# Output projection of a gated delta rule: two heads summed in PSUM, transposes moved from TensorE to a DMA

## The reference, cut to what matters

```python
H, DK, DV = 16, 96, 192
_, o = jax.lax.scan(step, S0, xs)          # o: (B, T, H, DV)
gate = (hidden_states @ Wg).reshape(B, T, H, DV)
var = jnp.mean(o * o, axis=-1, keepdims=True)
o = o * jax.lax.rsqrt(var + EPS) * norm_weight * jax.nn.silu(gate)
return o.reshape(B, T, VAL_DIM) @ Wo       # (B, T, 3072) @ (3072, 512), added to x
```

## Time and profile before

| | busy, us | share of the span |
|---|---|---|
| PE | 2216.2 | 96% |
| PE weight loads | 1536.5 | 66% |
| DVE | 2069.4 | 90% |
| ACT | 1463.5 | 63% |
| POOL | 1061.0 | 46% |
| DMA (share of the 16 engines) | | 20.3% |

### The profile page before, as it was taken

The page is one execution under the profiler, slowest core; times in us unless marked ns, Lnnn a source line. Parts: engine busy times, 40 slices in busy tenths (PEclk is TensorE's granted clock), DMA queues, the critical chain, the costliest instruction groups (busy, mean ns, idle before and its releaser), DMA issues. The chain is left out here.

```text
span 2311.0 us, 60628 instructions
## 1 busy us (share of the span) xinstructions
PE 2216.2 (96%) x22433; PEld 1536.5 (66%) x22456; DVE 2069.4 (90%) x4515; ACT 1463.5 (63%) x4019; POOL 1061.0 (46%) x1542
## 2 busy tenths in 40 slices
PE   5899999999999999999999999999999999888998
PEld 3576767676776767676767676767677676763554
DVE  8899999999999999999999999999999989567886
ACT  4566666666666666767677677766656566424665
POOL 3535445444535454545454544544443545224564
PEclk9999999999999999999999999999999999897999
DMA  5212222222222222222222222221111111021000
GB/s 140 61 39 55 54 58 51 58 55 55 53 53 55 53 50 60 65 66 64 59 60 51 64 61 67 58 66 39 39 36 35 23 34 23 18 87 59 21 24 28
DMA packets 289411, 121.07 MB, mean 52 GB/s; under 512 B 211510, under 2 KB 267094, under 8 KB 288604
## 3 DMA queue, kind: packets, MB, share of 16 engines
q1 hardware_dynamic: 289116, 117.19, 19.7%
HBM read 85.40 MB, written 31.74 MB: 51 GB/s over the span
## 5 line engine op out<-in xcount | busy, mean ns | idle before, releaser
L1445 DVE SCALAR_TENSOR_TENSOR d_y<-bank,d_cw,d_y 128x508 f32<-128x508 f32 (+2 forms) x576 | 421.4, 732 | 6.2 <-ACT d_y L1199 1.3
L791 POOL TENSOR_SCALAR d_ms<-d_sso 128x4 f32<-128x4 f32 x64 | 14.6, 228 | 573.9 <-ACT d_junk L1338 573.9
L740 POOL TENSOR_TENSOR d_Gm<-cst,gh 128x512 f16<-128x512 f32 x128 | 130.6, 1041 | 184.5 <-DVE d_ohl L1614 184.4
L1619 DVE SCALAR_TENSOR_TENSOR x<-bank,x 128x512 f32<-128x512 f32 x256 | 172.1, 677 | 47.3 <-PE bank L1012 47.3
L1199 ACT ACTIVATE d_y<-bank,d_cw 128x512 f32<-128x512 f32 x192 | 131.1, 684 | 77.6 <-PE bank L857 75.3
L1323 ACT ACTIVATE d_thg<-bank 128x384 f32<-128x384 f32 x128 | 62.3, 487 | 178.9 <-PE bank L967 176.6
L821 POOL TENSOR_SCALAR d_K<-d_tok,d_Em 128x96 f32<-128x96 f32 x256 | 156.9, 628 | 0.1
L1206 ACT ACTIVATE d_th<-d_y 128x512 f32<-128x512 f32 x192 | 121.8, 635 | 46.2 <-DVE d_y L1451 35.2
L775 POOL TENSOR_TENSOR d_V<-d_tok,d_kinv 128x640 f32<-128x640 f32 (+1 forms) x128 | 125.8, 1003 | 41.9 <-issue 39.1
L1248 ACT ACTIVATE d_tok<-bank 128x384 f32<-128x384 f32 x256 | 125.7, 491 | 24.3 <-PE bank L873 20.6
L1466 DVE SCALAR_TENSOR_TENSOR d_yv<-d_th,d_y 128x512 f32<-128x512 f32 x128 | 89.0, 696 | 52.7 <-ACT d_th L1206 44.5
(11 more groups left out here) (340 smaller groups left out, 6881.5 us busy)
## 6 DMA issues: line engine op xcount, KB each, us to landing
lt_blocks<-d_LT SPq DMA_DIRECT2D x64, 256.0 KB, 2.5
d_fw<-turned_gate_w SPq DMA_DIRECT2D x32, 256.0 KB, 3.2
d_XT<-x_blocks SPq DMA_DIRECT2D x128, 64.0 KB, 2.4
d_X<-x_blocks SPq DMA_DIRECT2D x128, 64.0 KB, 2.4
d_fw<-turned_val_w SPq DMA_DIRECT2D x32, 256.0 KB, 3.1
d_fw<-turned_out_w SPq DMA_DIRECT2D x32, 256.0 KB, 2.8
d_st<-in_L_attn_Wg_dram SPq DMA_DIRECT2D x16, 384.0 KB, 3.9
ternary<-d_ft SPq DMA_DIRECT2D x48, 128.0 KB, 1.9
```

Of the source, the lines that this page charges most:

```text
L740: nc.gpsimd.tensor_tensor(Gm[:, w, :, :], over(U, 1, B), over(gh[:, w, n, :], 2, P), ALU.mult).then_inc(s["Gm_ready"], 1)
L1445: nc.vector.scalar_tensor_tensor(out=yy[:, :, tap:], in0=pp[:, :, 0:P - tap], scalar=cw[:, ds(st.kp, 1), t, 3 - tap], in1=yy[:, :, tap:], ...
L1619: nc.vector.scalar_tensor_tensor(out=xs, in0=bank[(4, 7, 6, 5)[i]][:, :], scalar=1.0 / (SO * SW), in1=xs, op0=ALU.mult, op1=ALU.add).then_ ...
```

## The change

Steps are paired. Two heads (2j and 2j + 1) share a chunk of output, and their 384 columns are cut in three groups of 128 instead of twice 128 + 64; both heads are summed in PSUM. A unit `u` is a pair of heads, a chunk and two of the four batches: 64 units in all, each 2 batches x 3 groups x 3 products = 18 matmuls and two adds of 128x512. `units(n)` says which are done in step n: none for n < 6, unit n - 6 for n = 6 to 59, two (54 and 55) in step 60, and two in each of the steps 61 to 64. `wo` holds three groups of rows instead of two, and is kept for a pair.

The transposes go by way of DRAM. `low` is one instruction now; SP's `store` writes `ohl` to `normed` after it, and `load` reads a unit back with one transposing DMA of 128 x 1536 f16 into `onT`, which now has two buffers. In steps 5 to 59 it loads the unit of the next step (unit 55 goes out at the start of step 60). From step 61 on, it loads both units of the same step, behind the store of that step. The 12 transposes on PE and the two copies on ACT are gone. To make room, POOL's product `UB` is written into `Em` directly.

```diff
-        "wo": [[sb(f"wo{q}{h}", [P, 2, D], F16) for h in "hl"] for q in range(2)],
-        "nw": sb("nw", [P, 2]),
...
         "img": [nc.dram_tensor(f"x_blocks{q}", (N_BLOCK * I_STRIDE,), F32).ap() for q in range(2)],
...
+def wo_rows(k):
+
+    return (0, P, slice(0, HB)) if k % 2 == 0 else (HB, 0, slice(HB, P))
+
+
+N_PAIR = H // 2
+PER_PAIR = 2 * CH
+LAST = NS - CH + 1
+
+
+def units(n):
+
+    if n < 6 or n > NS:
+        return []
+    if n >= LAST:
+        first = (N_PAIR - 1) * PER_PAIR + 2 * (n - LAST)
+        return [first, first + 1]
+    return [n - 6, n - 5] if n == LAST - 1 else [n - 6]
+
+
+def added(n):
+
+    return max((2 * u + 2 for u in units(n)), default=0)
+
+
+def loads(n):
+
+    if n >= LAST:
+        return units(n)
+    return units(n + 1)[0:1] if n + 1 < LAST else []
+
+
+def stored_at(u):
+
+    return PER_PAIR * (u // PER_PAIR) + CH + 1 + u % PER_PAIR // 2
 
 
...
                         src = src.rearrange("(b x) -> b x", b=B)[:, at:at + HB * HB].rearrange("b (p e) -> p b e", p=HB)
                         sp.dma_start(tile, src).then_inc(s["X_loaded"], 16)
 
+            def store(n):
+
+                k, c = (n - 1) // CH, (n - 1) % CH
+                past(sp, "low_ready", n)
+                for q in range(2):
+                    past(sp, f"onT_in{q}", 16 * CH * (k // 2 - 1))
+                dst = oh[k // 2 % 2][c].rearrange("p (g h v) -> p g h v", h=2, v=DV)[:, :, k % 2, :]
+                sp.dma_start(dst, ohl[:, :, :, :].rearrange("p b l v -> p (b l) v")).then_inc(s["oh_out"], 16)
+
+            def load(u):
+
+                c, half = u % PER_PAIR // 2, u % 2
+                past(sp, "oh_out", 16 * stored_at(u))
+                past(sp, "wo_done", 2 * u - 2)
+                w = 2 * 6 * P
+                sp.dma_start_transpose(onT[u % 2][:, :, :], oh[u // PER_PAIR % 2][c][:, half * w:(half + 1) * w]).then_inc(s[f"onT_in{u % 2}"], 16)
...
                     gather(st)
-                    for place in range(2):
-                        for i in done_jobs(st, place):
-                            next_weights(i + 1)
+                    for i in done_jobs(st, 0):
+                        next_weights(i + 1)
+                if st.output:
+                    store(st.n)
+                    for u in loads(st.n):
+                        load(u)
+                if st.turn:
+                    for i in done_jobs(st, 1):
+                        next_weights(i + 1)
                     scatter(st)
...
-                nc.gpsimd.tensor_tensor(UB[:, :, :], over(cst[:, C_NU:C_NU + P], 1, B), over(Dn[:, :], 2, P), ALU.mult).then_inc(s["kappa_done"], 1)
+                past(pool, "PT_ready", m - 1)
+                nc.gpsimd.tensor_tensor(Em[q][:, :, :], over(cst[:, C_NU:C_NU + P], 1, B), over(Dn[:, :], 2, P), ALU.mult).then_inc(s["kappa_done"], 1)
...
-                past(pool, "PT_ready", m - 1)
-                nc.gpsimd.tensor_tensor(Em[q][:, :, :], E[:, :, :], UB[:, :, :], ALU.mult).then_inc(s["Em_ready"], 1)
+                nc.gpsimd.tensor_tensor(Em[q][:, :, :], E[:, :, :], Em[q][:, :, :], ALU.mult).then_inc(s["Em_ready"], 1)
...
-            def turn_output(st, part):
+            def output(st):
 
                 n = st.n
-                past(pe, "low_ready", n)
-                if part == 0 and st.turn:
-                    past(pe, "LT_ready", B * n + 2 * B)
-                if part == 1 and st.recur:
-                    past(pe, "W_ready", B * n + 4)
-                for e, g in enumerate(((0, 1), (2,))[part]):
-                    for i in range(B):
-                        last = nc.tensor.transpose(bank[6 - part][:, :].bitcast(F16)[:, (e * B + i) * P:(e * B + i + 1) * P],
-                                                   ohl[:, i, g, :], idh[:, :])
-                last.then_inc(s["onT_done"], 1)
-
-            def output(st, i):
-
-                n = st.n
-                if i == 0:
-                    past(pe, "onT_ready", 2 * n - 1)
-                    past(pe, "wo_ready", 2 * st.k + 2 if st.c else 2 * st.k)
-                if i < 2 and st.recur:
-                    past(pe, "qs_read", B * n + 2 * i + 2)
-                if i < 2 and not st.recur:
-                    past(pe, "gate_ready", 2 * n - 1 + i)
-                wh, wl = wo[st.wn]
-                terms = [(onT[:, 0, i, :], wh[:, 0, :]), (onT[:, 0, i, :], wl[:, 0, :]), (onT[:, 1, i, :], wh[:, 1, :]),
-                         (onT[:, 1, i, :], wl[:, 1, :]), (onT[:, 2, i, :], wh[:, 0, :])]
-                for e, (o, w) in enumerate(terms):
-                    if i == 0 and e == 4:
-                        past(pe, "onT_ready", 2 * n)
-                    last = nc.tensor.matmul(bank[(4, 7, 6, 5)[i]][:, :], o, w, start=(e == 0), stop=(e == len(terms) - 1))
-                last.then_inc(s["wo_done"], 1)
+                for e, u in enumerate(units(n)):
+                    past(pe, f"onT_in{u % 2}", 16 * (u // 2 + 1))
+                    past(pe, "wo_ready", 4 * (u // PER_PAIR) + 4)
+                    wh, wl = wo[u // PER_PAIR % 2]
+                    for i in range(2):
+                        at = (6, 5, 7, 4)[2 * e + i]
+                        if at == 6 and st.turn:
+                            past(pe, "LT_ready", B * n + 2 * B)
+                        if at == 5 and st.recur:
+                            past(pe, "W_ready", B * n + 4)
+                        if at == 7:
+                            past(pe, *(("qs_read", B * n + 4) if st.recur else ("gate_ready", 2 * n)))
+                        if at == 4:
+                            past(pe, "gate_ready", 2 * n + 1 if st.recur else 2 * n)
+                        for w in range(3):
+                            high, low = onT[u % 2][:, 6 * i + w, :], onT[u % 2][:, 6 * i + 3 + w, :]
+                            nc.tensor.matmul(bank[at][:, :], high, wh[:, w, :], start=(w == 0), stop=False)
+                            nc.tensor.matmul(bank[at][:, :], high, wl[:, w, :], start=False, stop=False)
+                            last = nc.tensor.matmul(bank[at][:, :], low, wh[:, w, :], start=False, stop=(w == 2))
+                        last.then_inc(s["wo_done"], 1)
 
             def turn_x(at):
                 past(pe, "tail_done", 3 * NS)
-                past(pe, "x_added", B * (NS - 3 + at))
...
-                if st.output:
-                    turn_output(st, 0)
-                    turn_output(st, 1)
                 for part in range(4 if c == 0 else 0, 6):
                     proj(2, part, 6)
-                if st.output:
-                    for i in range(B):
-                        output(st, i)
+                if len(units(n)) < 2:
+                    output(st)
...
                 gates(st, 0)
+                if len(units(n)) == 2:
+                    output(st)
...
-                past(pe, "x_added", B * n - 1)
+                past(pe, "x_added", added(n - 1) + 1 if units(n) else 0)
...
-                past(pe, "x_added", B * n)
+                past(pe, "x_added", added(n - 1) + 2 if units(n) else 0)
...
-                    past(a, "onT_done", 2 * n - 2)
-                    nc.scalar.activation(ohl[:, :, :, :].rearrange("p b g t -> p b (g t)")[:, :, 0:DV], on[:, :, :],
-                                         ACT.Copy).then_inc(s["high_ready"], 1)
-
-                def read_onT(part):
-                    past(a, "onT_done", 2 * n - 1 + part)
-                    past(a, "wo_done", B * n - B)
-                    w = (2, 1)[part]
-                    nc.scalar.activation(onT[:, 2 * part:2 * part + w, :, :].rearrange("p g b t -> p (g b t)"),
-                                         bank[6 - part][:, :].bitcast(F16)[:, 0:w * B * P], ACT.Copy).then_inc(s["onT_ready"], 1)
+                    past(a, "oh_out", 16 * (n - 1))
...
                     v.wait_ge(s["high_ready"], n)
-                    past(v, "onT_done", 2 * n - 2)
-                    flat = ohl[:, :, :, :].rearrange("p b g t -> p b (g t)")
-                    nc.vector.tensor_tensor(ohl[:, :, 2, :], on[:, :, 0:P], ohl[:, :, 0, :], ALU.subtract)
-                    nc.vector.tensor_tensor(flat[:, :, DV:2 * P], on[:, :, P:DV], flat[:, :, P:DV], ALU.subtract).then_inc(s["low_ready"], 1)
+                    past(v, "oh_out", 16 * (n - 1))
+                    nc.vector.tensor_tensor(ohl[:, :, 1, :], on[:, :, :], ohl[:, :, 0, :], ALU.subtract).then_inc(s["low_ready"], 1)
 
                 def add_x(i):
-                    v.wait_ge(s["wo_done"], B * (n - 1) + i + 1)
-                    xs = x_sb[:, i * CH + (c - 1) % CH, :]
-                    nc.vector.scalar_tensor_tensor(out=xs, in0=bank[(4, 7, 6, 5)[i]][:, :], scalar=1.0 / (SO * SW), in1=xs,
+                    u = units(n)[i // 2]
+                    v.wait_ge(s["wo_done"], 2 * u + i % 2 + 1)
+                    xs = x_sb[:, (u % 2 * 2 + i % 2) * CH + u % PER_PAIR // 2, :]
```

(17 more changed lines are left out.)

90 lines of the change are left out of this document (46 added, 44 removed).

## The result

The changed kernel takes 2282.16 us (median of 4 runs, 2281.15 to 2283.09) against 2311.39 us of the kernel before on the same chip (4 runs, 2301.46 to 2312.84). The ratio is 0.9884, with a 95% interval of 0.986 to 0.9908. Predicted were 2259 us, a range of 2236 to 2300, and 0.81 for faster. The direction and the range hold, but the time lies 2 us above the forecast's own, narrower range of 2238 to 2280. Of the forecast gain of 54 us, 29 came by the medians; the profiled execution has a span of 2279.8 us, 31.2 under the 2311.0 of before.

A forecast was written before the change was run, and what follows sets the result against it. PE was taken to set the pace, with DVE close behind. From 2312.8 us, the terms -58.9 - 16 + 16 - 17 + 11 + 2 + 9 = -54 gave 2259 us, range 2236 to 2300.

The forecast's parts named there:

- PE's work: Steps 6 to 59: no 12 transposes and 18 output matmuls instead of 20 save PE 1.09 us a step, -58.9 us.
- the adds' waits: Steps 6 to 59: PE no longer waits for the third and fourth add to x, -16 us, bounds 0 and 18.
- the rival in which DVE takes over: Steps 6 to 59: none of the second add's lateness falls into slack, +45 us instead of +16, 2288 us; chance 0.17.
- the wait that comes: Steps 6 to 59: DVE's second add waits for 18 matmuls, so DVE is late for PE; +16 us, bounds 0 and +45.
- Steps 60 to 63: Two units a step: +2.79 us each for PE, +11 us, and +2 us for the late load in steps 61 and 62.
- Step 64: Exposed end: 7.7 us for store and load, then 36 matmuls and the last add, 18.1 us; +9 us, bounds +6 and +12.
- Steps 1 to 5: No output there now: 27.2 us a step instead of 30.57, -17 us, bounds -12 and -25.
- The transposing load: Steps 5 to 59: taken as 3.9 us, landing before it meets the scatter, so it costs nothing.
- The collision: Transposing load still running when the scatter starts, delaying each of 54 steps; 2702 us at the far end; chance 0.14.
- The rival of a load of just 15.6 us: A load four times the plain one's delays each step by 1.0 us, 54 us in all: 2313 us, no change; chance 0.05.

The follow-up runs named there:

- the kernel with old data: Kernel after, but in steps 61 to 64 the transposing loads go out at the step's start and read another, finished buffer: 2262.0 us.
- the fourfold kernel: Kernel after, but the transposing loads of units 2 to 53 are each done four times, one after another: 2618.3 us, ratio 1.1315.

## Why the prediction was right and what it missed

**Right, by its own reasons: faster, because PE sets the pace.** The terms for PE's work and for the adds' waits gave -74.9 us; the kernel without the second add shows -74.7. That the two agree so closely is partly luck: that kernel has an add less than the sum assumes, and by the kernel before without two adds the waits were worth 22.7 instead of 16, which leaves 52.0 for PE's 58.9. In the steps of chunk 3 the distance fell by just 1.10 us (30.43 to 29.33) once the late add was gone, for 1.09 worked out. The total is not what the sum said: 2282 lies 23 us from the forecast of 2259 and 6 from the 2288 of the rival in which DVE takes over, and the range holds it because it was widened to take that rival in.

**Wrong in size: the wait that comes.** The step that failed is "+16 us" for the later second add. It measured 29.4 us, 0.54 a step for 0.3: per step 0.85 us in chunk 0, where I had 0.35, 0.14 in chunk 1, 0.45 in chunk 2 and 0.74 in chunk 3. I had found the place, the direction (DVE late at `y16`) and about the lateness of the add (1.06 us; the step read has 1.07, but behind 0.51 at the first add, so the agreement is partly luck). What I had not found is that first wait, of an add that now stands for nine products instead of five; and I let 0.6 us of slack in each step take the lateness, of which little was there. At the output pairs, where I expected nothing, PE waits for 15.8 us in all. The truth lay between my 16 and the 45 of the rival that DVE takes over; the same list in another order gives 2263 us, so 15.7 of the 29.4 us are the order. That rival was right for the steps of chunk 0, which hold 11.3 of the other 13.7.

**Steps 60 to 63, up to the end of `low` in 64: 21 us for 13.** The 16 products more were worked out (2.79 us a step). What I left out is line 1062's wait for the gate, 4.5 us in 3 pieces: the second unit's products go to banks 7 and 4, and DVE frees bank 4 only when `gate_pair(0)` is done, to which it comes behind two adds. The load in the same step cost 0.7 and 3.1 us in steps 61 and 62 (the 17.2 us of its wait less the 13.5 of step 64), for +2.

**Step 64: right.** 7.4 us for store and load (7.7), 18.8 us to the last add (18.1), +9.8 for +9. Thirteen products and not seven stood at the lower clock (0.50, 0.42 us apart); from the first product to the end of the last add it is 11.4 us for 10.4. The 20 us of the kernel with old data are no measure of what store and load cost, since there the products of step 64 run ahead of `low` too: theirs are 7.4 us in step 64 and the 3.7 us of waits in 61 and 62. No kernel that computes the right thing was tried for these.

**Steps 1 to 5: right.** 27.5 us a step for 27.2, and PE is no longer full: 129.3 of 137.6 us, at a granted clock of 0.99.

**The transposing load: right, and its rivals wrong.** Guessed 3.9 us for lack of a row, measured 4.5 (median), and hidden even when done twice. The collision, to which I gave 0.14, did not come; it takes more than two loads, 4.1 us each to landing in that run, and four cost 336 us. The rival of a load of just 15.6 us, four times the plain one's 3.9, was my estimate; no row of before shows such a factor. The trace of the kernel after has 4.5 us for the twelve blocks against 4.0 for a plain load of the same size, 1.1 times.

**Not in the forecast: the lower clock behind a wait.** I priced the collision by the time waited alone. In the fourfold kernel the waits for `X` are 3.4 of the 6.5 us that a step lost; PE's busy time rose by 187 us in steps 6 to 59, at a granted clock of 0.88 where the kernel after has 1.00.
